# A decoder's first cross attention: its key matrix split, its first context tiles normed and one of them turned inside the end of the state space ahead of it

## What is computed

```python
x = x + state_space_0(layernorm(x))                     # 16 states, 512 channels
x = x + cross_attention_0(layernorm(x), ctx, ctx)       # 16 heads of 64
x = x + experts_0(layernorm(x))
x = x + state_space_1(layernorm(x)); x = x + cross_attention_1(...); x = x + experts_1(...)

def cross_attention_0(Q, K, V):
    q = l2norm(heads(LN(Q, g, b) @ wq)); k = l2norm(heads(LN(K, g, b) @ wk)); v = heads(LN(V, g, b) @ wv)
    out = (q @ k.T) @ v          # no softmax: k.T @ v can be made first
    ...
```

## Time and profile before

| | before |
|---|---|
| time, median of 3 runs | 2791.53 us (2781.52 to 2801.99) |
| the profiled execution | 2788.32 us, its span 2786.6 us |
| PE busy | 2273.9 us (82%) |
| DVE busy | 2078.5 us (75%) |
| ACT busy | 1595.8 us (57%) |
| POOL busy | 1158.2 us (42%) |
| chain that ended last | PE 43%, ACT 18%, DVE 17%, POOL 11%, issue 8% |

### The profile page before, as it was taken

How to read it: one execution, slowest core, us unless ns; L and a number is a source line. 1 busy time by engine, 2 the same in 40 slices (tenths; PEclk the granted TensorE clock), 3 DMA queues, 4 the chain that set the end, 5 groups by cost and what they waited for, 6 DMA issues and landing times.

```text
span 2786.6 us, 36083 instructions
## 1 busy us (share of the span) xinstructions
PE 2273.9 (82%) x12948; PEld 1788.5 (64%) x12948; DVE 2078.5 (75%) x3066; ACT 1595.8 (57%) x2780; POOL 1158.2 (42%) x821
## 2 busy tenths in 40 slices
PE   5878875679998798959995688886679888899997
PEld 3565664557776687848883455655434445799997
DVE  5988989689996465547985889889656453577775
ACT  6777775346664445517883877775214444376762
POOL 3999999100000534210221799999502233100003
PEclk8888977889999799979997889788869886899999
DMA  4033040750000100013421330330264410266642
GB/s 179 10 113 114 9 147 0 258 196 1 24 1 0 37 1 31 16 67 108 175 88 47 121 122 2 121 99 35 47 104 100 98 50 23 101 218 225 209 170 87
DMA packets 101620, 247.57 MB, mean 89 GB/s; under 512 B 9285, under 2 KB 65361, under 8 KB 94274
## 3 DMA queue, kind: packets, MB, share of 16 engines
q1 hardware_dynamic: 88530, 222.43, 25.0%
q0 software_dynamic: 5376, 14.70, 1.6%
q10 hardware_dynamic: 7536, 8.13, 1.1%
HBM read 187.96 MB, written 48.81 MB: 85 GB/s over the span
## 4 chain that ended last, share of the span: by engine, by line
PE 43%; ACT 18%; DVE 17%; POOL 11%; issue 8%; DMA 1%; SPq 1%; ACTq 1%; POOLq 1%; another core or an unknown queue 0%; DVEq 0%
POOL bu L383 7%; PE psum L111 6%; PE psum L112 6%; PE psum L113 6%; PE psum L507 3%; PE psum L118 3%; ACT WH L3575 2%; ACT psum L631 2%; ACT g L3722 2%; PE psum L477 2%; POOL ch L407 2%; PE psum L457 2%; PE psum L453 2%; PE psum L485 2%; PE psum L3016 1%
## 5 line engine op out<-in xcount | busy, mean ns | idle before, releaser
L383 POOL TENSOR_TENSOR bu<-u,row 128x1024 f32<-128x1024 f32 x254 | 595.4, 2372 | 91.7 <-DMA row<-Ascr 44.9
L807 DVE TENSOR_TENSOR_SCAN psum<-psum,bu 128x1024 f32<-128x1024 f32 x176 | 402.1, 2285 | 43.6 <-ACT psum L631 38.4
L507 PE MATMUL psum<-ident,ch 128*128 128x128 f32 x2048 | 315.3, 314 | 43.7 <-POOL ch L407 36.0
L507 PEld LDWEIGHTS psum<-ident,ch 128*128 128x128 f32 x2048 | 284.5, 165 | 97.4 <-issue 41.3
L631 ACT ACTIVATE psum<-dt,A 128x511 f32<-128x511 f32 x512 | 332.5, 682 | 0.4
L824 DVE TENSOR_TENSOR ch<-psum,row 128x1024 f32<-128x1024 f32 x176 | 214.9, 1221 | 6.6 <-PE psum L507 2.2
L407 POOL TENSOR_TENSOR ch<-ch,row 128x1024 f32<-128x1024 f32 x80 | 189.2, 2365 | 25.8 <-DVE ch L807 25.6
L807 DVE TENSOR_TENSOR_SCAN ch<-psum,bu 128x1024 f32<-128x1024 f32 x80 | 181.7, 2279 | 5.5 <-PE psum L507 3.5
L3722 ACT ACTIVATE g<-psum,bias 128x256 f32<-128x256 f32 x248 | 100.8, 470 | 147.3 <-PE psum L113 126.2
L3544 POOL DMA_INDIRECT R<-m1res,gi x26 | 25.8, 991 | 349.8 <-DMA m1res<-ob 324.1
L111 PE MATMUL psum<-WH,hs 128*128 128x256 f32 x496 | 145.7, 294 | 10.3 <-DVE hs L3802 6.8
(11 more groups left out here) (458 smaller groups left out, 6717.0 us busy)
## 6 DMA issues: line engine op xcount, KB each, us to landing
W<-in_m1W SPq DMA_DIRECT2D x24, 2052.0 KB, 8.6
row<-Ascr SPq DMA_DIRECT2D x64, 512.0 KB, 5.0
row<-Bscr SPq DMA_DIRECT2D x64, 512.0 KB, 6.1
m1buf<-zt SPq DMA_DIRECT2D x8, 2048.0 KB, 17.2
W<-in_m0W SPq DMA_DIRECT2D x16, 1024.0 KB, 5.8
m1res<-ob ACTq DMA_DIRECT2D x23, 256.0 KB, 5.0
m0buf<-zt SPq DMA_DIRECT2D x2, 2064.0 KB, 17.9
xe<-m0buf SPq DMA_DIRECT2D x8, 516.0 KB, 8.3
```

Source lines behind the costliest of these rows:

```text
L383: e.tensor_tensor(m.bu[n % RING_B][:, :, :], u, m.row[:, g, 0, :, :], ALU.mult).then_inc(*m.fed.up)
L507: p = pe.matmul(m.y[:, c, :], m.ch[i % RING_C][:, j, 128 * c:128 * c + 128], k.ident, start=False, stop=g == UNITS - 1 and j == 1 and c == ...
L807: dve.tensor_tensor_scan(flat(to), flat(decays), flat(inputs), 0.0, ALU.mult, ALU.add).then_inc(*m.scan.up)
```

## The change

The keys stage's four engine functions become generators that give way (`yield`) at set places, and the state space's functions call them on (`next(keys)`) near their end.

- ACT rounds `wk` and takes the context's deviation after its last decay, ahead of its last copy `yt`; it rounds tile 0 behind that copy, ahead of the barrier.
- POOL subtracts `wk[1]` right behind its last `ch`, ahead of the barrier; its memset of `zt` comes after.
- DVE takes the three tiles' statistics and norms tiles 0 and 1 between its last `ch` and its last gate, and makes tile 0's rests behind the gate, ahead of the four additions to x.
- The statistics of x's last batch leave the state space's end: DVE's go to turn 3 of the keys loop, ACT's to turn 4, the inverse deviation to turn 5.
- PE turns tile 0 between its last `yt` and `out`.
- SP asks for the ten further context tiles ahead of the barrier.
- ACT and POOL first wait until units 121 to 123 (the last to use `row` 1 to 3) have made their `ch`. The semaphores used across the barrier are new ones; `gT` is allocated further ahead, which moves the small tiles behind it.

State space B is called without keys and keeps its statistics (`if m.rnd`).

```diff
+def mamba_rows_met(m):
+    return [mamba_out(m, PER * B - UNITS + g) for g in (1, 2, 3)]
...
 def mamba_pe
     mamba_item_pe(k, m, pe, "yt", B - 1, 3)
+    next(keys, None)
     for j in range(4):
         mamba_item_pe(k, m, pe, "out", B - 1, j)
...
 def mamba_act
+    next(keys, None)
     mamba_item_act(k, m, act, "yt", B - 1, 3)
-    x_stats_act(k, act, 4 * (m.rnd + 1) + B - 1)
+    next(keys, None)
+    if m.rnd:
+        x_stats_act(k, act, 4 * (m.rnd + 1) + B - 1)
...
 def mamba_dve
+    next(keys, None)
+    next(keys, None)
     mamba_gate_dve(k, m, dve, 4 * B - 1)
+    next(keys, None)
     for j in range(4):
         mamba_item_dve(k, m, dve, "out", B - 1, j)
-    x_stats_dve(k, dve, 4 * (m.rnd + 1) + B - 1)
-    x_inverse_dve(k, dve, 4 * (m.rnd + 1) + B - 1)
+    if m.rnd:
+        x_stats_dve(k, dve, 4 * (m.rnd + 1) + B - 1)
+        x_inverse_dve(k, dve, 4 * (m.rnd + 1) + B - 1)
...
 def keys_dve
     ahead = keys_normed_dve(k, m, dve, 0, seen[0])
+    next(ahead)
+    yield
+    while not seen[0]:
+        next(ahead)
+    yield
     turned(0, ahead)
+    yield
...
             drawn(i - 2)
+            if i == 3:
+                x_stats_dve(k, dve, 4 + B - 1)
+            if i == 5:
+                x_inverse_dve(k, dve, 4 + B - 1)
...
 def keys_act
     act.wait_ge(*m.w_k(0))
+    for rows_met in met:
+        act.wait_ge(*rows_met)
     act.copy(m.wk[0], m.wq[:, :, :]).then_inc(*m.wk_hi.up)
     ahead = keys_normed_act(k, m, act, 0, seen[0])
+    while not seen[0]:
+        next(ahead)
+    yield
     turned(0, ahead)
+    yield
...
+            if i == 4:
+                x_stats_act(k, act, 4 + B - 1)
...
 def keys_first_sp
+    keys_context_sp(k, m, sp, 0, 3)
...
+def keys_first_pool(k, m, pool, met):
+    for rows_met in met:
+        pool.wait_ge(*rows_met)
+    pool.wait_ge(*m.w_k(0))
+    pool.wait_ge(*m.wk_hi(0))
+    pool.tensor_tensor(m.wk[1], m.wq[:, :, :], m.wk[0], ALU.subtract).then_inc(*m.wk_lo.up)
```

More of the change, by code:

```diff
@@ L509, in mamba_sum_pe, with mamba_pe @@
     p.then_inc(*m.summed.up)
-def mamba_pe(k, m, pe):
+def mamba_pe(k, m, pe, keys=iter(())):
     for w, j in FIRST:
@@ L632, in mamba_decay_act, with mamba_act @@
     e.then_inc(*m.decay.up)
-def mamba_act(k, m, act):
+def mamba_act(k, m, act, keys=iter(())):
     L = m.L
@@ L764, in mamba_home_dve, with mamba_dve @@
     x_stats_dve(k, dve, 4 * m.rnd + b)
-def mamba_dve(k, m, dve):
+def mamba_dve(k, m, dve, keys=iter(())):
     if m.rnd:
@@ L871, in keys_make @@
     m.mt_zero = c("mT_zeroed", 1)
[L872 to L877, removed]
+    m.ctx_in = [first_in, c("context1", 4, 16)]
     m.k_rows, m.k_out = c("keys", tiles), c("keys_drawn", tiles)
@@ L1283, in keys_heads_act, with keys_act @@
         yield
-def keys_act(k, m, act):
+def keys_act(k, m, act, met):
     n_tiles = B * ST
@@ L1415, in keys_sp @@
         .then_inc(*k.cleared["m0"].up)
[L1416 to L1421, removed]
+    keys_context_sp(k, m, sp, 2)
+    keys_context_sp(k, m, sp, 3)
+def keys_first_pool(k, m, pool, met):
+    for rows_met in met:
+        pool.wait_ge(*rows_met)
     pool.wait_ge(*m.w_k(0))
@@ L1424, in keys_pool @@
     pool.tensor_tensor(m.wk[1], m.wq[:, :, :], m.wk[0], ALU.subtract).then_inc(*m.wk_lo.up)
+def keys_pool(k, m, pool):
+    pool.memset(k.zt[:, :, :], 0.0).then_inc(*m.zeros.up)
     pool.memset(m.mT[:, :, :], 0.0).then_inc(*m.mt_zero.up)
@@ L3904, in build @@
         k.early0 = [c("early_wk", 1, 16), c("early_context", 1, 16), c("early_ln_rows", 2, 16)]
+        k.keys0 = [c("early_wk_high", 1), c("early_wk_low", 1), c("early_context_mean_var", B + 2), c("early_context_dev", B + 2)] \
+            + [c("early_context_" + n, B * ST) for n in ("normed", "turned", "turned_high", "turned_low", "high", "low")] \
+            + [c("early_context_in", 4, 16)]
         k.early2 = [c("early_m0W1", 1, 16), c("early_m0W2", 1, 16)]
@@ L3973, in _ @@
             mamba_pool(k, mA, pool)
+            keys_first_pool(k, x0, pool, mamba_rows_met(mA))
             barrier(k, pool, 0)
@@ L3991, in _ @@
             act.wait_ge(*k.pv_in(0))
-            mamba_act(k, mA, act)
+            keys = keys_act(k, x0, act, mamba_rows_met(mA))
+            mamba_act(k, mA, act, keys)
             barrier(k, act, 0)
-            keys_act(k, x0, act)
+            for _ in keys:
+                pass
             barrier(k, act, 1)
@@ L4012, in _ @@
             dve.wait_ge(*k.consts(3))
-            mamba_dve(k, mA, dve)
+            keys = keys_dve(k, x0, dve)
+            mamba_dve(k, mA, dve, keys)
             barrier(k, dve, 0)
-            keys_dve(k, x0, dve)
+            for _ in keys:
+                pass
             barrier(k, dve, 1)
@@ L4029, in _ @@
             pe.wait_ge(*k.consts(3))
-            mamba_pe(k, mA, pe)
+            keys = keys_pe(k, x0, pe)
+            mamba_pe(k, mA, pe, keys)
             barrier(k, pe, 0)
-            keys_pe(k, x0, pe)
+            for _ in keys:
+                pass
             barrier(k, pe, 1)
```

22 lines of the change are left out of this document (11 added, 11 removed).

## The result

The changed kernel's median is 2773.25 us over 10 runs (2760.77 to 2782.58), against 2789.84 for the kernel before (10 runs, 2777.58 to 2801.99). The ratio is 0.9941, 95% interval 0.9921 to 0.9962: **16.5 us faster, with 10.6 and 22.0 as bounds**. The forecast was 8.9 faster. The time lies in the forecast range, and the change is within 1% as forecast, but the forecast gain lies outside the measured interval. The profiled execution of after took 2775.81, that of before 2788.32: 12.5 apart.

What follows compares the result with a forecast made beforehand. It took the keys stage to be bound by its chain of 52 tiles, PE and DVE nearly abreast, so an earlier first keys moves its end. −7.4 − 2.6 + 1.1 = −8.9 us gave 2782.6, range 2772 to 2796.

Steps and rivals of the forecast that it cites:

- The gate, +2.1: State space's end: statistics of three tiles and four normings on DVE start its last gate 2.1 us later, at 496.6.
- The split hidden, the norming not stopped: Ahead of the barrier: POOL's split ends at 494.4, 0.3 us before DVE's first norming, which then takes 0.48, not 4.45.
- Tile 0's turning, +0.1: PE between yt and out: turning tile 0 costs 0.1 us, bounded by 0 and 0.6.
- the clock, +1.7: PE's output product: after a 2.9 us wait, one stretch at half speed costs 1.7 us, ends 0 and 7.2.
- The first keys' start, −7.4: Start of the keys stage: first keys begin at 508.4 instead of 515.78, 7.4 us sooner.
- The first keys, −2.6: First keys on PE: at full speed they take 2.8 us instead of 5.43, ends 0 and −2.7.
- clock stays down: Rival: PE's half speed lasts through product and first two keys, net +2.4 us, 2793.9; chance 0.07.
- The statistics in turn 3, +1.1: Keys loop, DVE: moved statistics cost 1.65 us less a 0.51 wait, net 1.1; ends 0 and 1.65.
- SP and POOL, nothing: Early issue of ten context tiles by SP and POOL's later memset of zt cost nothing.
- given back: Rival: something else sets the keys stage's end, which stays where it was, 2791.5; chance 0.12.
- Beyond the stage, nothing: Stages behind the keys stage: the forecast had no term there.
- more: Rival: clock holds through the product (−1.7) and statistics vanish in a DVE wait (−1.1), −11.7 us, 2779.8; chance 0.15.

Runs made afterwards that it cites:

- e6: Changed kernel with DVE's norming partly behind the gate and PE's turning of tile 0 inside the product; first kn at 16.52, stage's end 0.15 us sooner than the changed kernel.
- e4: Changed kernel with only the key matrix's rounding and split (and context load) ahead of the barrier, norming, turning and statistics moved back; 14.5 us faster than before by ratio.
- e2: Changed kernel plus sixteen unread identity turnings on PE ahead of the last turning for yt; last addition at 14.61 instead of 15.84, last kn 0.3 us sooner.
- e1: Changed kernel with the statistics of x's last rows put back ahead of the barrier; ratio to before 0.9952, last kn 3.5 us later than the changed kernel.
- e5: Changed kernel with only POOL's split of the key matrix put back behind the barrier; 9.5 us faster than before by ratio, last kn at 395.06.
- e3: Changed kernel with the ten further context tiles asked for behind the barrier again; first kn 19.50 and last kn 384.68 us after the last ch, unmoved.
- e9: Kernel before with the changed kernel's new semaphores and place of gT, and zt zeroed behind the split; ratio to before 0.9993.
- e0: The changed kernel once more, unaltered; ratio to before 0.9936, or −17.8 us.

## Why the prediction was right, and where it wasn't

**The gate, +2.1.** Measured +1.96 (3.30 to 5.26). The rows were read rightly: 2.27 of statistics with root and four normings. e6 takes it away and gets all of it back at the first keys, 3.0 together with the clock. The gate starts at 497.00, right at the bound that the prediction set for being wrong. But `ch` had started 0.53 later than before, and counted from it the gate came 0.1 sooner than forecast. What the prediction didn't have is that these 2 us, with the clock's 1.2, count for 0.15 at the stage's end.

**The split hidden, the norming not stopped.** Split until 494.96, norming at 495.16 and 0.48 long. The margin was 0.2 where 0.3 was forecast. e4 confirms the price that was at stake, 4.0 (0.48 there in place of 4.45).

**Tile 0's turning, +0.1, and the clock, +1.7.** The last addition moved by 3.19, of it 1.96 by the gate: 1.23 was left where 1.8 was forecast. e2 shows that 1.23 is the clock and the turning nothing, for it turns tile 0 as well and reaches 14.61. The row used for the clock was the right one: 0.56 and 0.76 granted over twice 2.5 us are 3.4 us at half speed, and the earlier trace rows had 3.65. But part of these 3.4 fell on the waits around ACT's copy, where a slow clock costs nothing. The two terms together were over-sized by 0.57.

**The first keys' start, −7.4.** Measured −8.20. The difference is the gate's 0.14, the 0.57 of clock and turning, and a tenth at the barrier.

**The first keys, −2.6.** 3.13 instead of 5.43: −2.3, at full speed and 0.53 behind the start of DVE's last addition, where within 0.5 was forecast. e1 and e5 show the other case, with waits of 2.82 and 5.19 ahead of the keys. The rival "clock stays down" did not come about; e1 shows that it wasn't far: 2.2 us more of wait sufficed to put two thirds of the keys at half speed.

**The statistics in turn 3, +1.1.** Here the net effect was forecast wrongly, though not by the statistics' own price. DVE in after:

```profile
535.50 0.41 DVE L1189 TENSOR_TENSOR cs<-XF,cs 128x256 fp32r<-128x256 f32 x1
535.83 1.40 DVE L131 BATCH_NORM_STATS2 xst<-X 128x6 f32<-128x256 f32 x4
537.15 0.36 DVE L135 BATCH_NORM_AGGREGATE xmv<-xst 128x2 f32<-128x6 f32 x4
537.43 1.19 DVE L1235 TENSOR_REDUCE rn<-sq 128x16 f32<-128x1024 f32 x1
```

That turn's sum of squares, forecast about 9 before 547.10, came 9.7 before it, 10.2 counted from the last `ch`. So only 0.3 of the head start of 10.5 was gone there. `kn` of tile 3 had come 12.0 sooner, more than the 10.4 and 10.5 of its neighbours. The reason stands in PE's rows: the wait ahead of `g_tile(0)`, 2.58 before, is 1.78 in after, and no fall of the clock follows it.

```profile
527.14 0.41 PE L118 MATMUL psum<-ident,XF 128*128 128x128 f32 x2 [1.78 <-DVE XF L1131]
...
528.08 0.40 PE L111 MATMUL psum<-ks,cs 128*128 128x512 f32 x1
```

Two things meet in that turn, and other runs part them. In e5 and e6 the clock does fall behind that wait, as before, and there the statistics cost 1.05 and 1.02 between the sums of turns 2 and 3 (leads over before of 3.19 and 2.14, 13.31 and 12.29). That is the 1.1 of the forecast, since they replace the wait of 0.51. In e4 the clock does not fall (wait of 1.70) and the statistics are not there. Its lead grows by 0.83, from 3.47 to 4.30, and DVE's wait ahead of `vnT`, 0.90 before and 0.91 in e6, is gone:

```profile
532.74 0.42 DVE L1189 TENSOR_TENSOR vnT<-psum,vnT 128x256 fp32r<-128x256 f32 x1 [0.91 <-ACT vnT L1323]
```
```profile
540.09 0.42 DVE L1184 TENSOR_TENSOR vnT<-psum,vnT 128x256 fp32r<-128x256 f32 x1
```

(The first row is e6's, the second e4's.) The two together make −0.2, and after's lead went from 10.39 to 10.20. The term of 1.1 was thus right, and a gain of 0.8 beside it was missing: that the clock's fall of the earlier trace rows could go away is what the prediction had not asked. It used those rows for a price and left them where they were. The wait of 1.78 is shorter than 2.58 because the third keys, up to 524.86, ran at half speed throughout, so that PE was done later; in e1, where they ran at full speed, it is 4.03.

**SP and POOL, nothing.** e3 and e9 confirm it.

**The stage.** −10.1 for −8.9: the −0.8 of the first keys' start, the +0.3 of the keys themselves and the −0.8 of turn 3 make −10.2. The mechanism was right. The clock's term was too large, and the fall of the clock that went away was not in the sum. The rival "given back" fell for this change, whose end has moved by what its start has, but e2, e5 and e6 show it to be a live one: 1.2, 3.4 and 3.0 us of lead ended as 0.3, 0 and 0.15.

**Beyond the stage, nothing.** This is where the forecast failed, by about 6.4 of the 7.6 us that it missed. Its sum ended at the last `kn`, and no rival put anything behind it: the one named "more" (−11.7) holds two terms of the stage. The runs show an offset of about −6.4 for after and of −5 to −10 for e0 to e6, each known to some 5 us. It was also too wary of the scatter: twelve alternating runs of either kernel give the ratio to 0.2%, so the range could have been narrower around a better centre.

## What to carry to other kernels

Price a head start at the first link of a long chain, then ask what the new order does to the waits that already stand in the chain: here a clock fall 30 us later went away and gave back 0.8 of the 1.0 that moved statistics cost, while in variants 3 us of lead were lost on the way, in part where a stretch at half clock fell in another turn. Before a small instruction is put ahead of a gate, see how long the matmul engine waits at it: 2.6 us of wait cost 1.2 more in clock, and sixteen idle matmuls took that back, though only 0.3 of it reached the stage's end. Where a few us count, compare medians of some ten alternating runs, since one profile of this kernel can't place a difference of 6 us in a stage that itself varies by 17.

## What the runs showed of the hardware

In some places the granted clock came down about a microsecond behind the end of a wait. Matmuls resumed at full speed at 511.05 behind 2.82 us of wait, and were at half speed from 512.08 (e1). In e6 the second keys resumed at 509.89, behind 1.83, and fell to half speed at about 510.9. In other places they were slow from the first one on: in after the turning behind the wait of 2.62 took 1.09 instead of 0.63. The same 32 records of the product took 7.17 behind a wait of 1.09 and 7.96 behind one of 2.62.

The length of a wait does not tell it alone. In after, behind waits of 1.94 (up to 518.11) and 1.40 (up to 520.02) with half a microsecond of turning between them, the third keys ran at half speed from the first on. In e1, behind waits of 1.92 and 1.51 at the same place, they ran at full speed. Ahead of `g_tile(0)` a wait of 1.78 (after) had no fall behind it, and waits of 1.97 (e5), 2.58 (before) and 4.03 (e1) had one.

One stage with the same instructions, and the same work on DVE, ACT and POOL within 2 us, lasted 332 to 351 us between its barriers. In the stretches shown, 354 to 371 long, it goes in step with a mean granted clock of 0.82 to 0.77. That scatter is larger than the whole change.
